# The two normed rows of a tile formed on ScalarE instead of VectorE

## What is computed

```python
def _layernorm(x, axis=-1, eps=1e-05):
    m = jnp.mean(x, axis=axis, keepdims=True)
    v = jnp.var(x, axis=axis, keepdims=True)
    return (x - m) / jnp.sqrt(v + eps)

h = embeddings of the token and of its category, side by side      # 64 x 128 x 256
h = h + linear_attention(_layernorm(h))     # phi(q) (phi(k)^T v) / (phi(q) sum phi(k)), phi = elu + 1, 16 heads
h = h + experts(_layernorm(h))              # a gate picks among 16 experts, then causal attention, then output
```

## Time and profile before

| | before |
|---|---|
| median of 3 runs | 1187.47 us (1186.08 to 1189.19) |
| profiled execution | 1176.88 us |
| its span, first to last instruction | 1175.0 us |
| granted TensorE clock, mean | 0.973 |
| busy in the span: TensorE, VectorE, GpSimd, ScalarE | 1029.2, 928.9, 754.4, 533.6 us |
| busy from 35 to 442 us (407 us): the same | 375.0, 375.4, 296.3, 174.6 us |

### The profile page before, as it was taken

The page is one execution under the profiler, slowest core; times in us unless marked ns, Lnnn a source line. Parts: engine busy times, 40 slices in busy tenths (PEclk is TensorE's granted clock), DMA queues, the critical chain, the costliest instruction groups (busy, mean ns, idle before and its releaser), DMA issues.

```text
span 1175.0 us, 26735 instructions
## 1 busy us (share of the span) xinstructions
PE 1029.2 (88%) x6571; PEld 862.2 (73%) x6572; DVE 928.9 (79%) x3134; ACT 533.6 (45%) x1455; POOL 754.4 (64%) x975
## 2 busy tenths in 40 slices
PE   1999999999999993599999959999999999999898
PEld 0565656565666662588988849999999889988897
DVE  3789999999999996245544528999888888888898
ACT  3544444444433431234443425555555555555554
POOL 6657777777777756700000037888888888888785
PEclk9999999999999995799999979999999999999999
DMA  5642333333222225576777752333333333333230
GB/s 141 201 151 88 100 104 99 104 95 100 77 86 86 80 75 197 180 231 221 239 223 232 224 177 77 95 91 91 90 90 89 89 89 89 89 89 89 85 93 32
DMA packets 108096, 143.28 MB, mean 122 GB/s; under 512 B 15388, under 2 KB 95330, under 8 KB 107876
## 3 DMA queue, kind: packets, MB, share of 16 engines
q1 hardware_dynamic: 88004, 91.17, 24.4%
q0 software_dynamic: 18880, 50.36, 15.0%
q10 hardware_dynamic: 1152, 1.05, 0.3%
HBM read 77.37 MB, written 72.46 MB: 128 GB/s over the span
## 4 chain that ended last, share of the span: by engine, by line
PE 40%; DVE 22%; POOL 18%; issue 13%; ACT 3%; DMA 2%; POOLq 1%; SPq 0%; DVEq 0%; ACTq 0%
PE bank L1366 8%; PE bank L1291 7%; PE bank L1293 7%; PE bank L1292 7%; PE bank L1298 5%; POOL row_y L747 5%; POOL qk_neg L732 2%; POOL x2T L732 2%; PE bank L1364 2%; DVE phi L1055 2%; POOL x2T L728 2%; POOL x2T L734 2%; POOL qk_neg L728 2%; DVE h L1075 1%; POOL sorted_x L674 1%
## 5 line engine op out<-in xcount | busy, mean ns | idle before, releaser
L1291 PE MATMUL bank<-wo_hi,split_lo 128*128 128x256 f32 x1024 | 302.8, 296 | 4.6 <-DVE qk_e L1228 2.2
L1292 PE MATMUL bank<-wo_lo,split_hi 128*128 128x256 f32 x1024 | 287.3, 281 | 0.0
L1293 PE MATMUL bank<-wo_hi,split_hi 128*128 128x256 f32 x1024 | 287.2, 280 | 0.0
L1291 PEld LDWEIGHTS bank<-wo_hi,split_lo 128*128 128x128 f32 x1024 | 194.5, 190 | 9.3 <-DVE qk_e L1228 4.6
L1366 PE MATMUL bank<-w_attn,x1T 128*128 128x512 f32 (+1 forms) x512 | 201.2, 516 | 0.0
L1292 PEld LDWEIGHTS bank<-wo_lo,split_hi 128*128 128x128 f32 x1024 | 194.5, 190 | 0.0
L1293 PEld LDWEIGHTS bank<-wo_hi,split_hi 128*128 128x128 f32 x1024 | 194.0, 189 | 0.0
L843 ACT ACTIVATE h<-bank,rwo 128x256 f32<-128x256 f32 x256 | 107.4, 471 | 126.8 <-PE bank L1293 99.5
L747 POOL DMA_INDIRECT row_y<-sorted_y,pair_now x128 | 128.4, 1003 | 36.3 <-issue 28.5
L1166 DVE TENSOR_TENSOR split_lo<-bank,split_hi 128x256 fp32r<-128x256 f32 x144 | 61.2, 425 | 104.2 <-ACT split_hi L812 103.0
L740 POOL COPY pair_now<-pair_at 128x2 uint32 (+1 forms) x64 | 13.1, 205 | 195.7 <-SPq L531 195.6
(11 more groups left out here) (223 smaller groups left out, 2516.0 us busy)
## 6 DMA issues: line engine op xcount, KB each, us to landing
sorted_y<-row_y SPq DMA_DIRECT2D x36, 384.0 KB, 3.1
sorted_y<-w_attn SPq DMA_DIRECT2D x36, 384.0 KB, 3.2
row_x<-sorted_x SPq DMA_DIRECT2D x72, 128.0 KB, 2.4
h_rows<-h SPq DMA_DIRECT2D x64, 128.0 KB, 1.8
row_x<-h_rows SPq DMA_DIRECT2D x64, 128.0 KB, 2.9
out_h<-row_x SPq DMA_DIRECT2D x64, 128.0 KB, 2.0
category_table<-in_L_tok_special_table SPq DMA_DIRECT2D x10, 623.0 KB, 5.0
phi<-sorted_x SPq DMA_DIRECT2D x36, 128.0 KB, 2.1
```

Source lines behind the costliest of these rows:

```text
L1291: pe.matmul(ps, left[1][c], right[0][c], start=(c == 0), stop=False)
L1292: pe.matmul(ps, left[0][c], right[1][c], start=False, stop=False)
L1293: last = pe.matmul(ps, left[0][c], right[0][c], start=False, stop=(c == n - 1))
```

## The change

VectorE no longer forms x1 and x2. After its gate piece it computes, for one row of roots, the two values `centers` = -mean x root, in one instruction on 128x2 elements. ScalarE forms x1 and x2 as root x h + centers, by two activations with a scale and a bias from SBUF. They stand at the head of ScalarE's lap, before qk_neg. The waits for an x2 buffer's scatter move with them to ScalarE, and VectorE's h2 gets a wait for the x2 that was read from the same buffer. The small buffer ids_rows_f, used only ahead of the first lap, is laid into qk_e.

```diff
--- before.py
+++ after.py
...
 MASKED = -1.0e30
 
 
-P1_STEPS = ["ln1_stats", "ln1_moments", "ln2_stats", "ln2_moments", "var_eps", "var_inv", "roots_in", "roots",
+P1_STEPS = ["ln1_stats", "ln1_moments", "ln2_stats", "ln2_moments", "var_eps", "var_inv", "roots_in", "roots", "centers",
             "x1_normed", "x1_turned", "x1_T", "qk_product", "v_product", "qk_negative", "qk_exp", "v_copied",
             "phi", "phi_q_turned", "kv_product", "phi_q_T", "kv_masked", "attn_sums", "attn_den", "attn_z",
             "attn", "h2", "x2_normed", "x2_turned", "x2_T", "logits_product"]
...
         moments = sb("moments", [P, N_ROOTS, 2, 2])
         roots_in = sb("roots_in", [P, N_ROOTS, 3])
         roots = sb("roots", [P, N_ROOTS, 3])
+        centers = sb("centers", [P, N_ROOTS, 2])
         var_inv = sb("var_inv", [P, 1])
         x1 = sb("x1", [P, C])
         x2T = sb("x2T", [P, C])
...
             act.copy(ones_r[:, :], ones[:, :]).then_inc(setup_a, 1)
 
             def step1(i):
+                tile = i.shift(4)
+                if tile.inside(B):
+                    t = tile.c
+                    after(act, "x1_turned", tile.shift(-1))
+                    after(act, "centers", tile)
+                    act.activation(x1[:, :], h[t % 8], ACT.Identity, scale=roots[:, t, 0:1],
+                                   bias=centers[:, t, 0:1]).then_inc(done["x1_normed"], 1)
+                tile = i.shift(1)
+                if tile.inside(B):
+                    t = tile.c
+                    scatter_done(act, t - N_X2)
+                    after(act, "centers", tile.shift(3))
+                    act.activation(x2[t % N_X2], h2[tile.p][:, :], ACT.Identity, scale=roots[:, t + 3, 1:2],
+                                   bias=centers[:, t + 3, 1:2]).then_inc(done["x2_normed"], 1)
                 tile = i.shift(3)
                 if tile.inside(B):
 
...
                 piece, g = (i.c - 3) % QUAD, (i.c - 3) // QUAD
                 if 0 <= g < GROUPS:
                     (experts_chosen, rows_counted, weights_formed, rows_placed)[piece](g)
-                if x1_tile.inside(B):
-                    t = x1_tile.c
-                    after(dve, "x1_turned", x1_tile.shift(-1))
-                    after(dve, "roots", x1_tile)
-                    dve.tensor_scalar(x1[:, :], h[t % 8], moments[:, t, 0, 0:1], roots[:, t, 0:1],
-                                      ALU.subtract, ALU.mult).then_inc(done["x1_normed"], 1)
-                if x2_tile.inside(B):
-                    t = x2_tile.c
-                    scatter_done(dve, t - N_X2)
-                    after(dve, "roots", x2_tile.shift(3))
-                    dve.tensor_scalar(x2[t % N_X2], h2[x2_tile.p][:, :], moments[:, t + 3, 1, 0:1],
-                                      roots[:, t + 3, 1:2], ALU.subtract, ALU.mult
-                                      ).then_inc(done["x2_normed"], 1)
+                if 0 <= i.c + 4 < N_ROOTS:
+                    row = i.c + 4
+                    dve.wait_ge(done["roots"], row + 1)
+                    dve.scalar_tensor_tensor(centers[:, row, :], moments[:, row, :, 0], -1.0, roots[:, row, 0:2],
+                                             ALU.mult, ALU.mult).then_inc(done["centers"], 1)
                 if phi_tile.inside(B):
 
                     after(dve, "qk_exp", phi_tile)
...
                                       ).then_inc(done["attn"], 1)
                     after(dve, "attn", attn_tile)
                     landed_half(dve, h2_stored, attn_tile.shift(-2))
+                    after(dve, "x2_normed", attn_tile.shift(-2))
                     dve.tensor_tensor(h2[attn_tile.p][:, :], h[attn_tile.c % 8], attn[:, :], ALU.add
                                       ).then_inc(done["h2"], 1)
                     after(dve, "h2", attn_tile)
```

More of the change, by code:

```diff
@@ L173, in build @@
         ids_rows = sb("ids_rows", [B, T], I32)
-        ids_rows_f = sb("ids_rows_f", [B, T])
         ids_f = sb("ids_f", [P, B])
@@ L271, in build @@
         acc_p = [x2T, qk_neg[:, 0:C]]
+        ids_rows_f = qk_e[0:B, 0:T]
         sneg = sb("sneg", [P, 1])
```

## The result

| | before | after |
|---|---|---|
| median | 1188.11 us (1186.08 to 1189.19, 4 runs) | 1294.51 us (1292.6 to 1295.75, 4 runs) |
| profiled execution, its span | 1176.88, 1175.0 us | 1295.31, 1293.5 us |
| mean of the 61 laps from the second phi on (VectorE's phi to phi, profiled) | 6.49 us | 8.26 us |
| granted TensorE clock, mean | 0.973 | 0.936 |

The change makes the kernel slower: the ratio is 1.0904, with a 95% interval from 1.0881 to 1.0927. The medians differ by 106.4 us. Forecast were 1297 us, a range of 1273 to 1325, and "slower" with 0.95.

The account below looks back on a forecast made before the run. VectorE was taken as full, at 92% busy in the first stage. Lap stretches +108.7, last tile +1.1, less 3, made +106; with 4 for the clock +110, giving 1297 us on the median of 1187.47; range 1273 to 1325.

Parts of the forecast that it names:

- The path: First stage, each lap: VectorE idle from centers to phi while ScalarE runs x1, x2, qk_neg, exponential; 2.52 us, bounds 2.20 to 2.70.
- The sum: First-stage loop: +108.7 us for centers-to-phi stretches, +1.1 for the last tile's phi, less 3 taken off; +106 before the clock.
- VectorE's own stretch from phi to the next head: VectorE's work in each first-stage lap: 354.8 us, 5.72 a lap, nearly all staying.
- The 3.5 us of line 1086: VectorE's 62 adds: slowdown of 3.5 us in all, put down to GpSimd's transfers, which a longer lap would let finish.
- The waits that were put at nothing: Scatter waits moved to ScalarE, and h2's added wait for x2 of two tiles earlier: no cost.
- the 4 us for the clock: TensorE's granted clock falls briefly in some first-stage laps after pauses of some 1.6 us; 4 us, up to 17.
- the upper bound of +121: First-stage loop's added time by the longer path length, 2.70 us; +121 us, before up to 17 for the clock.
- the term of 47.1: Kernel before: stretches from x1's start to phi's start on VectorE, added up lap by lap; 47.1 us.
- Rival B: TensorE's clock stays low for much of the first stage and sets the pace: +84 us on top, 1381; chance 0.07.
- TensorE's busy share: Sign that the forecast is right: TensorE busy some 73% of the first stage.
- ScalarE's idle time before x1: Sign that the forecast is right: some 3 us a lap on ScalarE in the first stage, put down to centers.
- rival A: The norms hide in ScalarE's idle time before qk_neg, TensorE bounds the lap: 7 us gained, 1180; chance 0.03.

Follow-up runs that it names:

- kernel 9: The changed kernel with x1 formed on VectorE again and only x2's norm on ScalarE, behind the exponential and v's copy: 1171.85 us, ratio 0.9946 to the kernel before.
- experiment 3: The kernel before plus two same-shaped activations on constants at ScalarE's head, with no wait for VectorE: 1186.4 us, ratio 1.0.
- experiment 1: The changed kernel with the two norms moved behind the exponential in ScalarE's lap, nothing else: 1195.55 us, ratio 1.0081 to the kernel before.
- kernel 8: The kernel before with v's copy ahead of x1T's on ScalarE, nothing else: 1172.58 us, ratio 0.9954.
- experiments 5, 7 and 10: Against the kernel before: both norms on ScalarE behind exponential and v's copy, TensorE reordered (1.0047) or not (1.0212); only x2's norm there, behind x1T, TensorE reordered (1.0052).
- experiment 2: The changed kernel with both norms back on VectorE, ScalarE keeping only the wait for centers at its head: 1227.35 us, ratio 1.0349 to the kernel before.

## Why the prediction came out right

**The path, point by point.** Predicted were 0.23 from centers to x1, 0.50 and 0.50 for the two activations, 0.63 to the exponential and 0.66 to phi, together 2.52 us. The lap shown above has 0.24, 0.51, 0.49, 0.61 and 0.66, together 2.51. Of the 62 laps 44 have 2.51 or 2.52; most others have 2.55 to 2.60, and one 2.81. Where 2.60 was seen (the lap at 339.25) centers itself took 0.21 instead of 0.15. The estimate of the activation from rows 8 and 9 (0.61 long, 0.51 apart) was as good as the path needed:

```profile
L775 ACT ACTIVATE x<-h,centers,roots x32: 599/600/602, 26.1 to 510.5; 128x256 f32<-128x256 f32 x32
...
L782 ACT ACTIVATE row_y<-h,centers,roots x36: 583/586/587, 46.8 to 542.8; 128x256 f32<-128x256 f32 x36
...
L1057 DVE SCALAR_TENSOR_TENSOR centers<-moments,roots x67: 147/154/231, 25.9 to 561.5; 128x2 f32<-128x2 f32 x67
```

The Trainium skill ("ScalarE: Activation LUTs", What ACT_TABLE_LOAD costs) gives a length that grows by about 93 ns with each pointer operand. By its figures this one is estimated at 585 ns, and the trace agrees, with 586 for the second of the pair and 600 for the first.

**The sum.** Added up over 62 laps, from the head (x1, now centers) to phi, there are 156.8 us against 47.1 before: +109.7, where +108.7 was predicted. VectorE's own stretch from phi to the next head was to stay, less 3 us. It stayed: 349.15 against 349.34 us over 61 laps. The 3.5 us of line 1086 did come back (its adds take 10.5 instead of 14.0 us), and the traces bear out the reason that was given: in the kernel before 44 of the 62 ran beside a scatter of GpSimd's (line 674) and took 249 ns on average, the others 169; in the changed kernel none does, and all take about 169. Two laps that the low clock lengthened took 3.3 us. Phi of the last tile starts at 552.02 instead of 442.30, 109.7 later. The waits that were put at nothing, for a scatter on ScalarE and for x2 ahead of h2, show none in the loop, and behind the rise of the clock in the second stage the rest takes 688.2 us, as against 687.7 before.

Three small slips stand in the sum. Its terms, 108.7 + 1.1 - 3, make 106.8, and with the 4 us for the clock +111, not +110. The terms of the path's bounds add up to 2.22 and 2.72, not 2.20 and 2.70. And the upper bound of +121 leaves out the 3 us that the sum takes off. None of them changes where the result lies in the range.

**The profiled execution and the median.** The two profiled executions differ by 118.4 us, the medians by 106.4. The loop accounts for 109.7. Another 8.4 lie between the last phi and the rise of the clock in the second stage, which takes 44.9 us in the profiled execution of before and 53.3 in that of after. These 8.4 come without the change too: the two profiles of kernel 9, one and the same program, have 45.6 and 54.5 there, and experiment 3, whose median is that of the kernel before, has 53.3. Over all thirteen profiles the stretch takes 44 to 47 or 52 to 55 us, whatever the kernel.

The loop varies too. The same two profiles of kernel 9 have laps of 6.32 and 6.47 us. In experiment 3, with laps of 6.58 us in its profile, the stretches from x1 to phi add up to 52.6 us, not 47.1; if that is what a usual execution of the kernel before has, the loop accounts for +104 and not for 109.7. That would more than explain why the medians differ by 3.6 us less than forecast: the term of 47.1 was taken from an execution 0.9% faster than the median, while the sum was put on top of the median. It isn't shown, since experiment 3 has two activations more and there is no profile of a usual execution of the kernel before. To this extent the nearness of 1297 to 1294.51 is luck; the path of 2.51 us is not.

**The clock.** Predicted: short falls in some laps, 4 us. The trace has 21 stretches at 0.50 within the loop, 99.0 us in all; before there was none. The longest kind looks so in windows:

```profile
288.00:291.00 3.00, 1.06 (x6) 0.67 (x7) 1.06 (x4) 2.67 (x7) 2.39 (x3) 1.00 0.25 75
291.00:301.00 10.00, 10.00 (x29) 6.81 (x28) 5.61 (x24) 3.02 (x7) 4.89 (x6) 0.51 0.26 80
301.00:304.00 3.00, 2.69 (x16) 1.78 (x15) 2.69 (x11) 1.60 (x5) 0.49 (x1) 0.91 0.21 64
```

TensorE is busy 1.06 of 3 us at full clock, then for 10 us at 1.2 GHz without a pause, then mostly at 2.4 GHz again. What it cost is read on VectorE and TensorE:

```profile
298.35 0.69 DVE L1062 SCALAR_TENSOR_TENSOR phi<-bank,qk_e 128x512 f32<-128x512 f32 x1 [2.36 <-issue]
300.64 0.17 DVE L1067 TENSOR_SCALAR den<-bank 128x16 f32<-128x16 f32 x1 [1.60 <-PE bank L1331]
...
393.51 3.65 PE L1374 MATMUL bank<-w_attn,x1T 128*128 128x512 f32 x4
...
396.64 0.15 DVE L1057 SCALAR_TENSOR_TENSOR centers<-moments,roots 128x2 f32<-128x2 f32 x1
```

In the lap around 298 VectorE's den waits 1.60 us for TensorE's sums: here, and once more at 497.58 with 1.48, a fall reaches the path. They are the two falls of 10.2 us. In the others, as at 393.51, the qk product takes 3.65 instead of 1.98 us and hardly anything on the path waits for it, since TensorE had slack in a lap of 8.26: centers at 396.64 comes 8.05 us behind the one before it, as it does four laps earlier at full clock (356.52 to 364.57). The 4 us were of the right size; that a third of the laps, 24 of 62, would be touched was not foreseen. Rival B had the falls and not their price. The Trainium skill ("TensorE: Matmul & The Clock Gate", HAM oscillation) tells of such falls behind waits of 3 to 5 us, once in every tile. The waits here are half as long or less, and most laps pass without a fall, so B did not hold in full, as the prediction had read that page; and that each fall costs the time of the slower clock, as it does there, the trace does not bear out where the engine waits anyway.

**Signs that were off.** TensorE's busy share was to be some 73%; it is 83%. TensorE was busy 98.2 of the 99.0 us at the lower clock; at full clock the same work is estimated at half, 49 us less, and the share at 73%. ScalarE's idle time before x1 was to be some 3 us a lap; it is 235.0 / 61 = 3.9 in the waits put down to centers. Neither carries a term of the sum. For rival A, experiment 1 shows how far it was: even with the place mended, the norms on ScalarE gave nothing back, and in the lap shown TensorE's turns follow ScalarE's x1, x2 and vx one by one. Of the 7 us that rival A hoped for from TensorE's lap, 5.4 came from the swap of two copies (kernel 8), which needs no work moved.

## What to carry to other kernels

Before work is moved to an engine with idle time, ask what that idle time waits for and what is queued behind the new wait. An engine with 43% busy time may still be the one whose next two instructions another engine needs at once; here a wait alone, without work, cost 3.5%, and the work alone cost nothing. Put an instruction with a late input behind those whose results are waited for, and when a queue is reordered, follow for each engine what it then waits for: the orders of experiments 5, 7 and 10, which looked free, turned one wait into another.

## What was not expected of the hardware

- TensorE's granted clock fell 21 times in 62 laps with a pause of up to about 1.5 us in each, by stretches of 3.4, 6.8 or 10.2 us, while most laps with the same pause passed without a fall. In experiment 2 there were 7 such stretches (23.9 us), in experiment 1 none.
- The same kernel's laps differ from execution to execution: kernel 9 had a mean lap of 6.32 us in one profile and 6.47 in the other, with the kernel before at 1178.0 and at 1187.1 us beside it. The recorded ratios were 0.9946 and 0.9947. A part of the difference between groups of runs lies at the start of the second stage: from the last phi to the rise of the granted clock there are 44 to 47 us in the five profiles of the groups with the kernel before near 1178, and 52 to 55 us in the six of those near 1187. Why is open.
- The second of two activations of one shape that follow each other took 586 ns in the median and the first 600. Why is open.
